# Sixteen attentions per head on one core: a second quarter of an exponential moved to VectorE in nine units, and VectorE's own work put last in every step

## The reference

```python
x = L0_attn_x                                   # (16, 256, 128)
xn = _layernorm(x, axis=-1)
x = x + attention(xn, Wq, ..., weights) + experts(xn, gate_w, w1, b1, w2, b2)

# attention: 16 heads of 8 columns, 16 "wavelengths" w
Qw, Kw = Q * cos(phase)[w, h], K * cos(phase)[w, h]
scores = einsum('bhqd,bhkd->bhqk', Qw, Kw) * SCALE
scores = scores * cos(KERR * scores * scores)
acc += einsum('bhqk,bhkd->bhqd', softmax(scores), V) * weight[w]
# then the mean over w, and Wo; the experts are a top-1 mixture of 8 with a capacity
```

## Time and profile before

| | us |
|---|---|
| median of 3 runs | 1752.14 (1751.83 to 1753.89) |
| the profiled execution | 1751.54 |
| its span, first to last instruction | 1749.8 |
| ScalarE busy | 1697.8 (97%) |
| VectorE busy | 1550.2 (89%) |
| TensorE busy | 1533.6 (88%) |
| GpSimd busy | 214.1 (12%) |

### The profile page before, as it was taken

One profiled execution on the slowest core, in us unless ns is written; L12 is line 12 of the kernel. 1 busy time (PEld: TensorE's weight loads), 2 busy tenths in 40 slices (PEclk: granted clock), 3 DMA queues, 4 the chain that ended last, 5 costly groups with the idle time before them and its releaser, 6 DMA issues.

```text
span 1749.8 us, 47130 instructions
## 1 busy us (share of the span) xinstructions
PE 1533.6 (88%) x20726; PEld 974.9 (56%) x20726; DVE 1550.2 (89%) x2310; ACT 1697.8 (97%) x517; POOL 214.1 (12%) x246
## 2 busy tenths in 40 slices
PE   8988888898888899999999998888888888887888
PEld 5555555555555566666666655555555555555555
DVE  5569799999988999999999998899999888998796
ACT  4899999999999999999999999999999999999996
POOL 4406100122110000000000000243330000000000
PEclk8999999999999999999999999999999999999999
DMA  4200000110001111011110000000000000000010
GB/s 123 97 19 16 15 5 32 51 53 25 26 9 36 37 44 44 16 30 44 44 44 23 14 11 15 25 25 26 26 10 15 16 15 15 16 11 6 2 28 27
DMA packets 45828, 49.71 MB, mean 28 GB/s; under 512 B 7565, under 2 KB 38325, under 8 KB 45621
## 3 DMA queue, kind: packets, MB, share of 16 engines
q1 hardware_dynamic: 42176, 42.11, 7.7%
q0 software_dynamic: 2048, 4.20, 0.8%
q10 hardware_dynamic: 1396, 0.33, 0.2%
HBM read 30.50 MB, written 15.73 MB: 26 GB/s over the span
## 4 chain that ended last, share of the span: by engine, by line
ACT 78%; PE 17%; issue 2%; DVE 1%; DMA 0%; POOL 0%; SPq 0%; DVEq 0%; POOLq 0%
ACT Pr L1435 76%; PE bank L1213 9%; PE bank L987 2%; ACT Pr L1428 2%; PE bank_b L1390 1%; PE bank L519 1%; PE bank L1363 1%; PE bank L1144 0%; PE bank L595 0%; PE bank L1128 0%; DVE negmax L1134 0%; PE bank L630 0%; PE bank L570 0%; PE bank L980 0%; PE bank L1616 0%
## 5 line engine op out<-in xcount | busy, mean ns | idle before, releaser
L1435 ACT ACTIVATE Pr<-T 128x4096 f32<-128x4096 f32 x463 | 1629.5, 3637 | 11.4 <-PE bank L1213 9.7
L1213 PE MATMUL bank<-Pr,Vst 128*32 128x256 f32 x14912 | 902.9, 382 | 191.5 <-ACT Pr L1435 106.5
L1213 PEld LDWEIGHTS bank<-Pr,Vst 128*32 128x32 f32 x14912 | 499.6, 109 | 476.6 <-issue 275.6
L1134 DVE TENSOR_REDUCE negmax<-bank 128x2 f32<-128x512 f32 x248 | 159.0, 682 | 55.2 <-PE bank L1128 54.7
L1150 DVE COPY T<-bank 128x512 f32<-128x512 f32 x248 | 168.8, 683 | 20.2 <-PE bank L1144 18.1
L1390 PE MATMUL bank_b<-terms,ident 128*128 128x128 f32 x992 | 143.7, 277 | 1.1 <-DVE terms L1375 1.1
L1356 DVE TENSOR_SCALAR pv_s<-bank,row_scale 128x512 f32<-128x512 f32 x192 | 142.2, 741 | 0.9 <-PE bank L1213 0.8
L1390 PEld LDWEIGHTS bank_b<-terms,ident 128*128 128x128 f32 x992 | 125.9, 191 | 12.3 <-issue 8.6
L1363 PE MATMUL bank<-ident,pv_s 128*128 128x128 f32 x768 | 117.3, 275 | 2.6 <-DVE pv_s L1356 2.6
L1371 DVE RECIPROCAL rsum<-bank 128x48 f32<-128x48 f32 (+1 forms) x192 | 79.8, 416 | 36.9 <-PE bank L1363 36.6
L1375 DVE TENSOR_TENSOR terms<-bank,rsum 128x384 f32<-128x384 f32 (+1 forms) x192 | 98.5, 513 | 6.6
(11 more groups left out here) (251 smaller groups left out, 1406.7 us busy)
## 6 DMA issues: line engine op xcount, KB each, us to landing
Ks<-qk_parts SPq DMA_DIRECT2D x30, 288.0 KB
Qs<-qk_parts SPq DMA_DIRECT2D x90, 96.0 KB
qk_parts<-work SPq DMA_DIRECT2D x12, 384.0 KB, 2.9
work<-in_L_ffn_w_dram SPq DMA_DIRECT2D x16, 256.0 KB, 3.8
dispatched<-d_both SPq DMA_DIRECT2D x5, 512.0 KB, 6.5
region<-dispatched SPq DMA_DIRECT2D x8, 320.0 KB, 4.0
expert_out<-work SPq DMA_DIRECT2D x8, 320.0 KB, 2.9
out_dram<-base SPq DMA_DIRECT2D x8, 256.0 KB, 3.0
```

What stands on the lines that cost most here:

```text
L1134: nc.vector.reduce_max(negmax[par][:, ds(p * QT, QT)], sc_bank[rr][:, :].rearrange("p (t k) -> p t k", k=SEQ), AX.X, negate=True).then_inc ...
L1213: ins = nc.tensor.matmul(bank[VC * j:VC * (j + 1), half * SEQ:(half + 1) * SEQ], Vst[par][:, at:at + VC], moving, start=opens and half == ...
L1435: nc.scalar.activation(Pr[n % RING][:, :], T[par][:, :], ACT.Exp, scale=scales[u % 2][w]).then_inc(exp_done, 1)
```

## The change

The third piece of VectorE grows from one quarter of wavelength 14 to two (2048 columns, as the other pieces) in the WIDE units 6 to 8 and 23 to 28; in 18 to 22 it stays a quarter (`last_tiles`). So VectorE does six quarters of wavelengths instead of five in nine units, and ScalarE two quarters instead of three of wavelength 14 there. `WIDE_OPS_AT` has a second row for those units. In every unit VectorE takes the maxima and the copies of T ahead of its own operations of the step. The 19 products of zeros are gone. The logits move to steps 0 to 3 of unit 1, and VectorE's copy of them from step 1 to step 4.

```diff
-    PIECES = ((W - 1, 0, 2), (W - 1, 1, 2), (W - 2, 0, 1))
+    PIECES = ((W - 1, 0), (W - 1, 1), (W - 2, 0))
...
             pe.wait_ge(const_ready, 3)
-            keep_clock(6, BANK)
-            pe.wait_ge(x_in[0], 16)
-            keep_clock(8, BANK)
-            pe.wait_ge(var_ready, 1)
-            keep_clock(5, SEQ)
             turn_x(0)
...
-                w, half, tiles = PIECES[i]
+                (w, half), tiles = PIECES[i], last_tiles(u) if i == len(PIECES) - 1 else 2
...
-                for c in range(PIECES[-1][2], 2 * QT):
+                for c in range(last_tiles(u), 2 * QT):
...
-            WIDE_OPS_AT = (1, 1, 0, 1, 0, 2, 1, 2, 1, 1, 1, 2, 3, 2, 0, 0)
+            WIDE_OPS_AT = {1: (1, 1, 0, 1, 0, 2, 1, 2, 1, 1, 1, 2, 3, 2, 0, 0),
+                           2: (1, 1, 1, 0, 0, 2, 1, 2, 1, 1, 1, 2, 2, 2, 1, 0)}
+
+            def last_tiles(u):
+
+                return 1 if EU + E <= u < EU + E + 5 else 2
...
-            LOGITS0_AT = {(0, 10): 0, (0, 13): 1, (0, 15): 2, (1, 0): 3}
+            LOGITS0_AT = {(1, 0): 0, (1, 1): 1, (1, 2): 2, (1, 3): 3}
...
                     for v, q in groups_at(COPY_AT, u, w):
                         dve_products(dve, v, q)
-                    deal = D_OPS_LAST if u == UNITS - 1 else WIDE_OPS_AT if kind == WIDE else D_OPS_AT[D_CHUNKS[u]]
-                    for i in range(sum(deal[:w]), sum(deal[:w + 1])):
-                        if kind == WIDE:
-                            dve_wide(dve, u, i)
-                        else:
-                            dve_d_exp(dve, u, par, i)
                     for v, no, p in scores_at(u, w):
                         dve_scores(dve, no, v % 2, p, p % 2)
                     for v, no, p in turns_at(u, w):
                         if u:
                             dve.wait_ge(exp_done, EXPS_BEFORE[u] + 1)
                         dve_transposed(dve, no, v % 2, p, p % 2)
+                    deal = D_OPS_LAST if u == UNITS - 1 else WIDE_OPS_AT[last_tiles(u)] if kind == WIDE else D_OPS_AT[D_CHUNKS[u]]
+                    for i in range(sum(deal[:w]), sum(deal[:w + 1])):
+                        if kind == WIDE:
+                            dve_wide(dve, u, i)
+                        else:
+                            dve_d_exp(dve, u, par, i)
...
-                        if w == 1:
+                        if w == 4:
                             dve_gate(dve, LOGITS0)
```

More of the change, by code:

```diff
@@ L515, in first_scores @@
                             ins.then_inc(first_made, 1)
-            def keep_clock(n, cols):
-                for _ in range(n):
-                    nc.tensor.matmul(banks[0][:, 0:cols], ident[:, :], zeros[:, 0:cols].bitcast(f32), start=True, stop=True)
             pe.wait_ge(const_ready, 3)
-            keep_clock(6, BANK)
-            pe.wait_ge(x_in[0], 16)
-            keep_clock(8, BANK)
-            pe.wait_ge(var_ready, 1)
-            keep_clock(5, SEQ)
             turn_x(0)
@@ L1426, in act_step @@
                 if w == W - 2 and KINDS[u] == WIDE:
-                    to, blocks = (t[:, :].rearrange("p (j b k) -> p j b k", j=GR, k=SEQ)[:, :, PIECES[-1][2]:, :] for t in (Pr[n % RING], T[par]))
-                    nc.scalar.activation(to, blocks, ACT.Exp, bias=LN_PIECE if PIECES[-1][2] % QT else 0.0, scale=scales[u % 2][w]).then_inc(exp_done, 1)
+                    to, blocks = (t[:, :].rearrange("p (j b k) -> p j b k", j=GR, k=SEQ)[:, :, last_tiles(u):, :] for t in (Pr[n % RING], T[par]))
+                    nc.scalar.activation(to, blocks, ACT.Exp, bias=LN_PIECE if last_tiles(u) % QT else 0.0, scale=scales[u % 2][w]).then_inc(exp_done, 1)
                     return
```

## The result

The changed kernel takes 1790.3 us (median of four runs, 1788.7 to 1791.3) against 1753.0 (1751.8 to 1754.3) for the kernel before on the same chip: ratio 1.0213, 95% interval 1.0200 to 1.0225. It is slower, as predicted, but by 37 us and not by 14: 1790.3 lies outside the range of 1754 to 1773. The profiled execution has a span of 1788.6 us, before 1749.8, so 38.8 us are to be found.

What follows compares the result with a forecast made beforehand. ScalarE, 97% busy, bounds the kernel before; in six-quarter units a chain through VectorE's copies would. 10.8 + 2.1 + 2.0 - 0.9 + 0 = 14.0 on 1752.1 gives 1766.1, said as 1766 us, range 1754 to 1773.

Steps and rivals of the forecast that it cites:

- The chain: Exponential 2 through VectorE's copies of step 5 and group 4 to the next exponential 2: 52.98 us against 51.78, nine units +10.8.
- The step that failed: Six-quarter unit's end: start of VectorE's copy of group 4 to end of TensorE's next step 0 products, 3.32 us from unit 23.
- GpSimd in units 20 to 22: VectorE's operations slowed beside GpSimd's combine; with slack down to 1.25 us, 0.7 lost per unit, +2.1 together.
- the 1.96 of unit 23: Two VectorE operations beside GpSimd's combine took 3.38 and 2.08 us instead of 2.28 and 1.22: 1.96 longer.
- The reorder elsewhere: VectorE's new order in the eight expert units: set at nothing, with 0.5 us each as upper bound.
- SIDE to QKV go with them: The unit kinds SIDE to QKV were treated like the expert units: nothing set for the new order.
- Unit 0 and the head: Start of the kernel: moved logits give -0.9 us in unit 0; removed zeros between -3.2 and +2.2, taken as 0.
- The 0.9 of the logits: Unit 0: TensorE's step 13 logits, 1.06 us ahead of tiles of T, go from there: -0.9 us.
- a slow head: Without the zeros, TensorE's first products run at the lower clock, the head 2.2 us longer; total given as 1769.
- ScalarE as the bound: Rival: VectorE's lateness is taken up, nine units give 7.7 us and unit 0 0.9: 1743.5; chance 0.08.
- VectorE's whole work of 51.35 as the bound: Rival: six-quarter units last 51.35 us by VectorE's total work, without the chain: 1749.3; chance 0.09.
- The third, costs in the expert units: Rival: the order costs 0.5 us more in each of eight expert units, plus a slow head: 1772; chance 0.08.

Runs made afterwards that it cites:

- e7_fill6: Changed kernel with six products on zeros on TensorE ahead of the turn of group 4 in the nine six-quarter units: 1778.1 us, ratio 1.0150.
- e13_max_ahead: Changed kernel with only the maxima ahead of VectorE's own operations, the copies of T behind them as before: 1762.5 us, ratio 1.0050.
- e14_copies_ahead: Changed kernel with only the copies of T ahead of VectorE's own operations, the maxima behind them as before: 1788.8 us, ratio 1.0203.
- e11_deal: Changed kernel with own operation 16 of a six-quarter unit at step 14, behind the copy of group 4, instead of step 13: 1779.0 us, ratio 1.0146.

## Why the prediction was right in its direction and wrong in its size

**The chain** was right. Its place, its waits (1.10 at the copy of step 5, none until the copy of group 4, 3.06 at TensorE) and its length of 52.98 us are in the trace, and `e7_fill6` runs at 52.93. That the copies and not the maxima carry it is shown by `e13_max_ahead` and `e14_copies_ahead`, that own operation 16 is a link of it by `e11_deal`.

**The step that failed** is "from the start of the copy of group 4 to the end of the products of the next step 0 ... 3.32". I took it from a place where TensorE waited 0.65 us and used it for one where it waits 3.06. After such a wait the turn and the products, or the products alone, ran in most units at 1.2 GHz: up to 4.94 in the steady unit. Eight six-quarter units besides 23 lost 21.5 us where 9.6 were predicted. Of the difference of 11.9, 10.6 are turns and products that took longer than the 2.51 of the earlier trace rows (by 2.2 in unit 6, 1.2 in 7, 1.0 in 8, nothing in 24, 1.5 to 1.6 in 25 to 28), and 1.0 are waits of 0.2 to 0.4 one exponential later, behind the slow products. The six filling products gave back 11, though units 20 to 22 took 1.6 more in that run. The prediction had the earlier trace rows with the 0.50 in view and used it for the head alone.

**GpSimd in units 20 to 22** was mis-sized: 8.8 instead of 2.1. I carried the 1.96 of unit 23 over as it stood. But the new order shifts VectorE against GpSimd, both long operations fall beside the combine with more of GpSimd's operations left to wait for (3.1 instead of 1.96), and the pass at step 12 needs them sooner than the copy of group 4 does; I had counted the slack at the end of the unit and not at the pass. In unit 23 the clock and GpSimd meet: 6.3 instead of 3.2, of which the turn and the products (1.12 and 3.64) are 2.2. Of the 25 us that the forecast missed, some 14 are thus the clock, some 8 GpSimd, and the rest the head and the units before 6.

**The reorder elsewhere**: right for the expert units (0.1 us in eight), wrong for "SIDE to QKV go with them": 2.3 us with the maxima ahead. Why VectorE's slack is smaller there was not tried.

**Unit 0 and the head**: a gain, of 2.9 us and not 0.9. The 0.9 of the logits came as forecast (ScalarE's bracket 0.86 instead of 1.75), 1.3 came in the head, which was put at 0 (its first exponential at 37.16 instead of 38.45), and the rest at other waits of unit 0. Without the zeros the turn started at 15.27 behind a tile of ScalarE's; the forecast had some 16.0, and its own give 15.6. (By its sum a slow head makes 1768, not 1769.) All this is worth nothing in the end, since units 1 and 2 take it back in either order. What holds those units to their time was not tried; the row before shows 1.11 us of it.

**The rivals**: ScalarE as the bound is excluded by the brackets of 3 us. VectorE's whole work of 51.35 as the bound fits the old order (51.45). The third, costs in the expert units, did not come.

## What to carry to other kernels

When a chain runs through an engine that must wait in it, price the work behind the wait also at the lower clock: look for a row of the same operation that follows an equally long wait. Ask of each operation moved forward what it waits for, and how much ready work now stands behind it; a maximum or copy that frees someone else's buffer is no reason to take it first if its input is not there. A contention read in one place holds only for the phase in which the two engines stood there; after a reorder it is to be worked out again, from what is left of the other engine's operation when this one starts, and against the first reader of the late result.

## What the runs showed of the hardware

- The same wait of 3.06 us left TensorE's clock at the upper level at the end of unit 24 (products 1.93 us, ScalarE's bracket 1.39) and at the lower one at the end of each of the next four (brackets 2.92 to 3.02). After waits of 1.93 us (`e11_deal`) it stayed up in four units and fell in four. Which of the two comes is not settled by the length of the wait alone, and what settles it was not tried.
- Two VectorE operations that start while a TENSOR_TENSOR of GpSimd runs lasted 1.5 to 1.6 us longer, within 0.14 the rest of GpSimd's operation. In the other case, where VectorE's operation had begun first (unit 20 before, 1144.48 to 1146.68), it kept its 2.28 us and GpSimd's took 3.48 instead of 1.90.
- Filler products inside a wait raised the speed of a kernel: six in each of nine units, 2.77 us a unit, took 11 us off the changed kernel.
- Without the products of zeros the first turn of x took 1.94 us for its eight parts and the first two projections 2.05, where it was 1.04 and 1.10 with them. The granted clock of that window (16 to 20 us) reads 1.00 all the same, so that this was the lower level is told by the durations alone and is not shown.

```profile
15.27 1.94 PE L494 MATMUL bank<-ident,region 128*128 128x128 f32 x8 [15.27 <-ACT region L387]
17.13 2.05 PE L502 MATMUL bank<-xnT,shared 128*128 128x512 f32 x2
```
